# The band mask of a windowed attention: laid into the score banks by ScalarE, in place of a matmul

## The reference, cut to what matters

```
q, k = l2norm(q) * qs, l2norm(k) * ksc            # 16 heads of 64
q, k = rotary(q), rotary(k)
mask = (it < jb) | (it > jb + w) | (jb == -1)     # window w = 32
sim  = where(mask, -max, (q @ k^T) * 8)
out  = softmax(sim) @ v
x    = out @ Wo + x
x    = ffn(shift_tokens(x)) + x
```

## Time and profile before

| | |
|---|---|
| median of 3 runs | 2150.25 us (2150.19 to 2153.46) |
| span of the profiled execution | 2147.6 us |
| PE busy | 2027.4 us (94%) |
| DVE busy | 1735.7 us (81%) |
| ACT busy | 1552.4 us (72%) |
| POOL busy | 1353.9 us (63%) |
| L367, the band matmul | 384 times, 149.7 us busy, 390 ns each |
| L633, the exponentials | 1536 times, 682.4 us busy, 454 ns each |

### The profile page before, as it was taken

One profiled execution on the slowest core, in us unless ns is written; L12 is line 12 of the kernel. 1 busy time (PEld: TensorE's weight loads), 2 busy tenths in 40 slices (PEclk: granted clock), 3 DMA queues, 4 the chain that ended last, 5 costly groups with the idle time before them and its releaser, 6 DMA issues.

```text
span 2147.6 us, 44268 instructions
## 1 busy us (share of the span) xinstructions
PE 2027.4 (94%) x14352; PEld 1593.7 (74%) x14352; DVE 1735.7 (81%) x3845; ACT 1552.4 (72%) x4966; POOL 1353.9 (63%) x1884
## 2 busy tenths in 40 slices
PE   7699999899999889999999999988999999999997
PEld 5477777777777767777777777776777777777776
DVE  4688887788888678888778888867888867888876
ACT  3488887378888558888738888846888864888873
POOL 2477666466766547777547666745766664766661
PEclk8799999999999999999999999999999999999999
DMA  3000000000000010000010000001000000000000
GB/s 98 30 9 0 0 0 1 17 36 1 0 0 0 11 35 9 0 0 0 1 44 9 0 0 0 0 11 35 9 0 0 0 4 11 1 0 0 0 0 20
DMA packets 11920, 21.08 MB, mean 10 GB/s; under 512 B 1659, under 2 KB 9518, under 8 KB 11054
## 3 DMA queue, kind: packets, MB, share of 16 engines
q1 hardware_dynamic: 11822, 19.77, 2.9%
HBM read 18.72 MB, written 1.05 MB: 9 GB/s over the span
## 4 chain that ended last, share of the span: by engine, by line
PE 68%; DVE 14%; ACT 7%; issue 6%; POOL 4%; DVEq 0%; DMA 0%; ACTq 0%; SPq 0%; POOLq 0%
PE ps L371 15%; PE ps L378 7%; PE ps L351 7%; PE ps L389 7%; PE ps L359 6%; ACT pr L633 6%; PE ps L397 5%; PE ps L353 5%; PE ps L352 5%; PE ps L367 3%; PE ps L520 3%; DVE nmax L966 3%; DVE xs L924 1%; PE ps L341 1%; DVE hT L1052 1%
## 5 line engine op out<-in xcount | busy, mean ns | idle before, releaser
L633 ACT ACTIVATE pr<-ps,nbias,rn 128x128 f32<-128x128 f32 x1536 | 682.4, 454 | 204.6 <-DVE nbias L970 199.4
L784 POOL TENSOR_TENSOR pr<-pr,rsum 128x512 f32<-128x512 f32 x384 | 395.4, 1039 | 304.0 <-DVE rsum L974 304.0
L759 POOL TENSOR_TENSOR t<-t 128x512 f32<-128x512 f32 x384 | 485.1, 1273 | 65.3 <-DVE t L950 59.1
L371 PE MATMUL ps<-kT,qT 64*128 64x128 f32 x3072 | 445.1, 285 | 0.0
L371 PEld LDWEIGHTS ps<-kT,qT 64*128 64x128 f32 x3072 | 371.6, 188 | 97.5 <-issue 97.5
L966 DVE TENSOR_REDUCE nmax<-ps 128x4 f32<-128x512 f32 x384 | 258.7, 674 | 67.2 <-PE ps L371 67.1
L633 ACT ACTIVATION_READ_ACCUMULATOR pr<-ps,nbias,rn 128x1 f32 x1536 | 306.3, 199 | 0.0
L351 PE MATMUL ps<-w_hi,xt_hi 128*128 128x512 f32 x576 | 280.5, 487 | 23.1 <-DVE t L950 18.1
L948 DVE TENSOR_TENSOR t<-ps,rope 128x512 f32<-128x512 f32 x384 | 261.2, 680 | 8.7 <-ACT sq L609 8.7
L950 DVE TENSOR_TENSOR t<-ps,rope 128x512 f32<-128x512 f32 x384 | 260.5, 678 | 0.0
L934 DVE TENSOR_REDUCE ss<-sq 128x8 f32<-128x512 f32 x384 | 248.8, 667 | 3.5 <-issue 2.6
(11 more groups left out here) (116 smaller groups left out, 3173.9 us busy)
## 6 DMA issues: line engine op xcount, KB each, us to landing
wqkv<-wqkv_in SPq DMA_DIRECT2D x6, 1536.0 KB, 8.4
wo<-wo_in SPq DMA_DIRECT2D x6, 512.0 KB, 3.6
w<-w_in SPq DMA_DIRECT2D x6, 342.0 KB, 3.0
w<-w_in SPq DMA_DIRECT2D x6, 172.5 KB
x<-x_in SPq DMA_DIRECT2D x4, 256.0 KB, 4.2
out<-x SPq DMA_DIRECT2D x4, 256.0 KB, 2.3
ctx<-ctx_in SPq DMA_DIRECT2D x4, 240.0 KB, 3.8
qks<-qk_scale_in SPq DMA_DIRECT2D x6, 64.0 KB, 2.8
```

The source lines that it names most:

```text
L371: i = mm(ps[:, o, k * P:(k + 1) * P], qT[r, par, h // 2, :], kT[r, par, h // 2, :], start=False, stop=k == 3, skip_group_check=True)
L633: i = A(pr[:, g, k, :], ps[:, S_BANK[g], k * P:(k + 1) * P], ACT.Exp, bias=nbias[:, g, k:k + 1], scale=rn[:, par, g // 2, 0, 2 * k + g % 2 ...
L759: G.tensor_tensor(t1[:, c, :], t1[:, c, :], t2[:, c, :], ALU.add).then_inc(qk_added[c], 1)
L784: G.tensor_tensor(w, w, rsum[:, g, :].unsqueeze(2).broadcast_to([P, 4, P]), ALU.mult).then_inc(pr_ready[g], 1)
```

## The change

The band becomes an fp32 tensor of 128 x 512, and the bf16 band and the bf16 identity go. The band matmul of each group goes. Instead ACT copies the band into the bank right behind the group's four exponentials, after waiting for their end, and signals `band_laid[g]`; the score matmuls then add to what lies in the bank. PE waits for `band_laid` where it waited for `exp_ready`. The first band of each of the two banks in a layer is laid by `lay_first_bands`: in layer 0 ahead of the first split of x, in the others between the table load and the last squares.

```
-    ident16 = sb("ident16", [P, P], BF16)
-    band16 = sb("band16", [P, 4, P], BF16)
+    band = sb("band", [P, 4, P])
...
             def scores(l, b, par, g):
                 u = g // 2
+                if first_element(b):
+                    pe.wait_ge(band_first, l * 2 + 2)
...
-                mm(ps[:, o, :], ident16[:], band16[:].rearrange("p a k -> p (a k)"), start=True, stop=False, skip_group_check=True)
...
-                    bank_free(pe, l, i, (exp_ready[0], 2))
+                    bank_free(pe, l, i, (band_laid[0], 2))
                     scores(l, i - 2, parity, 2)
...
+                if j == 0:
+                    pe.wait_ge(band_laid[2], nth(l, B - 1))
...
                 i.then_inc(exp_ready[g], 1)
+                act.wait_ge(exp_ready[g], nth(l, b))
+                lay_band(S_BANK[g]).then_inc(band_laid[g], 1)
+
+            def lay_band(bank):
+
+                return A(ps[:, bank, :], band[:].rearrange("p a k -> p (a k)"), ACT.Copy)
+
+            def lay_first_bands(l):
+
+                if not (isinstance(l, int) and l == 0):
+                    act.wait_ge(f_h, l * (NQ * FCH))
+                lay_band(S_BANK[0]).then_inc(band_first, 1)
+                lay_band(S_BANK[1]).then_inc(band_first, 1)
...
                     nc.scalar.preload_act_table_set("natural_log_exp_and_others")
+                    lay_first_bands(n)
                     square(n, 0, 0, Q1)
                     guess_norm(n, 0, 0, 0)
```

More of the change, by code:

```diff
@@ L171, in build @@
         sems(s, 4) for s in ("s_ps", "max_ready", "bias_ready", "exp_ready", "rsum_ready", "pr_ready", "pt_ps", "pt_ready"))
+    band_laid, band_first = sems("band_laid", 4), sem("band_first")
     o_ps, o_ready = sems("o_ps", 2), sems("o_ready", 2)
@@ L433, in step @@
                 if live(i, 1):
-                    bank_free(pe, l, i, (exp_ready[3], 2), (exp_ready[1], 2))
+                    bank_free(pe, l, i, (band_laid[3], 2), (band_laid[1], 2))
                     scores(l, i - 1, 1 - parity, 1)
@@ L459, in step @@
                 if live(i, 1):
-                    bank_free(pe, l, i, (exp_ready[2], 2), (exp_ready[0], 2))
+                    bank_free(pe, l, i, (band_laid[2], 2), (band_laid[0], 2))
                     scores(l, i - 1, 1 - parity, 0)
@@ L467, in step @@
                 if live(i, 1):
-                    bank_free(pe, l, i, (exp_ready[1], 1))
+                    bank_free(pe, l, i, (band_laid[1], 1))
                     scores(l, i - 1, 1 - parity, 3)
@@ L501, in ffn_up @@
                     pe.wait_ge(f_lo, l * NQ + q + 1)
+                if j == 0:
+                    pe.wait_ge(band_laid[2], nth(l, B - 1))
                 if j == 1:
                     pe.wait_ge(x_updated, nth(l, B - 1))
+                    pe.wait_ge(band_laid[3], nth(l, B - 1))
                 if j >= 2:
@@ L523, in _ @@
             pe.wait_ge(ld_const, 80)
-            pe.wait_ge(const_ready, 8)
+            pe.wait_ge(const_ready, 7)
             cross_transpose(0)
@@ L682, in _ @@
             act.wait_ge(ld_const, 80)
-            A(ident16[:], ident, ACT.Copy).then_inc(const_ready, 1)
-            act.wait_ge(const_ready, 8)
+            act.wait_ge(const_ready, 7)
             cross_copy_inputs(0)
@@ L716, in _ @@
             nc.scalar.preload_act_table_set("natural_log_exp_and_others")
+            lay_first_bands(0)
             copy_xt(0, 0, 0)
@@ L837, in _ @@
                     split_weights(0, c + 1)
-            pool.wait_ge(const_ready, 8)
+            pool.wait_ge(const_ready, 7)
             step(0, 0, 0)
@@ L1063, in _ @@
             dve.wait_ge(ld_const, 80)
-            V.tensor_copy(band16[:], consts[:, 0:P].unsqueeze(1).broadcast_to([P, 4, P])).then_inc(const_ready, 1)
-            dve.wait_ge(const_ready, 8)
+            V.tensor_copy(band[:], consts[:, 0:P].unsqueeze(1).broadcast_to([P, 4, P])).then_inc(const_ready, 1)
+            dve.wait_ge(const_ready, 7)
             cross_normalise_x(1)
```

## The result

The changed kernel takes 2188.64 us (median of 4 runs, 2186.94 to 2196.52), the kernel before 2150.7 (2150.19 to 2153.46): a ratio of 1.019, 95% interval 1.0167 to 1.0214. It is 38 us slower. The profiled spans, from the first to the last instruction, differ by 2187.4 - 2147.6 = 39.8 us.

What follows compares the result with a forecast made beforehand. A repeating chain over GpSimd and VectorE was taken as the bound: 0.62 - 0.30 = +0.32 us a step, times 84 is +26.9, with 1.5 for the seams +28.4: 2179 us, likely range 2163 to 2195, bounds 2146 to 2211.

Steps and rivals of the forecast that it cites:

- What bounds the kernel: A repeating chain through GpSimd's norm work and VectorE operations ending with it, 18.25 us a turn, rather than TensorE.
- The copy's price: On ScalarE between exps 0 and guess_norm 0, one band copy delays the guess by 0.62 us, bounds 0.33 to 0.71.
- The saving: Ahead of the scores of g 1, the removed band matmul takes 0.30 us off a step, between 0 and 0.39.
- The g 0 matmul buys nothing: Ahead of the nbias of g 0, removing that matmul gains nothing, since GpSimd's rotate Q0 holds until 625.46.
- The step: Between successive transposes of x: +0.32 us, 18.64 in place of 18.32.
- The seams: Between layers, the two first band copies delay the square of Q1: 0.29 us five times, +1.5 us.
- TensorE's new waiting: In each step, TensorE waits some 1.2 to 1.5 us more, mostly on the transpose of x and its consumers.
- TensorE alone as the pace: Across the whole step, TensorE's list sets the time, four band matmuls save 77 us: 2073 us, chance 0.09.
- no change: Between exps 0 and guess_norm 0, the copy costs only 0.33 us and cancels the saving: 2152 us, chance 0.08.
- The second copy on the turn: Behind exps 1, a copy delays pT of g 2 and costs 0.62 us more: 2230 us, chance 0.12.
- the one behind exps 3: On ScalarE, this copy pushes the split of x to 632.18, ahead of GpSimd's 632.39: a cover of 0.2 us.
- the port opens: The copy of x and clamp_norm slip in ahead of GpSimd's work; ScalarE's list sets 18.36 us: 2155 us, chance 0.09.

Runs made afterwards that it cites:

- pool_on: Kernel before plus one 128x128 GpSimd add a step, right behind refine_norm 0: 2170.84 us, step 18.59 us.
- pool_off: Kernel before plus one 128x128 GpSimd add a step, behind normalise_p 2 where GpSimd waits: 2154.07 us, step 18.34 us.
- pe_g1: Kernel before with the band matmul of group 1 issued twice: 2170.3 us, step 18.55 us.
- pe_g3: Kernel before with the band matmul of group 3 issued twice: 2154.25 us, step 18.37 us.
- norot: Kernel before with GpSimd's rotary adds for Q0 and K0 cut from 512 to 16 columns: 2131.95 us, step 18.12 us.
- lay0: Changed kernel with the band copied only behind the exponentials of g 0; the other three groups keep their matmul: 2197.83 us, step 18.99 us.
- lay3: Changed kernel with the band copied only behind the exponentials of g 3, for group 1; the other three groups keep their matmul: 2130.99 us, step 18.11 us.
- nomask: Changed kernel with the mask left out, neither band copies nor band matmuls: 2137.96 us, step 18.10 us.
- lay123: Changed kernel without the copy behind the exponentials of g 0; the scores of g 2 keep the band matmul: 2150.96 us, step 18.11 us.
- moved03: Changed kernel with the copy behind exps 0 moved behind guess_norm 0 and that behind exps 3 behind the next step's copy of v: 2145.28 us.
- moved0: Changed kernel with only the copy behind exps 0 moved, to behind guess_norm 0: 2160.79 us, step 18.21 us.

## Why the prediction was right, point by point

- **What bounds the kernel** was right: GpSimd's stretch, with the VectorE operations that end as it does, and not TensorE (pool_on against pool_off, pe_g1 against pe_g3, norot). That POOL works without a gap there holds in every other step only; the 0.17 us between them stand before and after alike and drop out of the difference.
- **The copy's price** was forecast at 0.62, the row of an ACT copy from PSUM to SBUF, and is 0.68 in the timeline, 0.65 in lay0. The term that was off is "the next one 0.48 after its start": behind the band copy it is 0.54. The destination is not shown to be the reason. The row taken reads PSUM, the band copy reads SBUF, and the trace of the kernel before has a plain ScalarE copy of this shape between SBUF tensors, which the prediction didn't use: the next operation starts 0.54 after it as well (the median of 24 such copies).
```profile
737.12 0.63 ACT L673 ACTIVATE xhT_hi<-xhT 128x512 fp32r<-128x512 f32 x1 [2.80 <-DVE xhT L1043]
737.66 0.67 ACT L680 ACTIVATE gate<-ps,vec 114x512 f32<-114x512 f32 x1
```
With it the price would have been 0.14 + 0.54 = 0.68. The estimate by the Trainium skill (ScalarE: Activation LUTs, section "What ACT_TABLE_LOAD costs") gave 0.66.
- **The saving** was forecast at 0.30 and is 0.24 in the timeline, 0.23 in lay3. It is the 0.23 that the chain gives the matmul, and not the distance of two starts, 0.32.
- **The g 0 matmul buys nothing**: right. What it brought, 0.23 beyond the g 1 saving, went into a longer nbias (0.70). Here the rule of the Trainium skill (SBUF — State Buffer, section "Who interferes with whom") that was weighed in the prediction decided the sign.
- **The step**: forecast +0.32, measured +0.42. Both terms were off by 0.06 in the same direction. The last ten steps' 0.416 times 84 is 34.9 of the 39.8 us, where the forecast had 26.9.
- **The seams**: forecast +1.5, and 4.9 is left for all that is outside the steps. 3.3 of it stands ahead of the first transpose of x (72.73 before, 76.04 now), but nomask, which has no copy, has 76.86 there, and lay0 73.91. From the last of the 14 transposes of a layer to the first of the next layer's, the five seams changed by -3.95, +2.45, -0.42, -0.57 and -1.43, so the forecast of +0.29 each can't be read from them. The term was not separated from the spread between runs and stays unshown.
- **TensorE's new waiting**: forecast 1.2 to 1.5 us a step, mostly on the transpose of x and its consumers; it is 1.3, of which 0.7 stands ahead of that transpose.
- **The rivals**: TensorE alone as the pace, 2073 us, is refuted; no change needed a price of 0.33, and it is 0.68. The second copy on the turn, the one behind exps 1, costs nothing in lay123 and moved03 (18.11); the one behind exps 3, which was to be covered by 0.2, costs the 0.10 between moved0 and moved03. The copy of x did slip in ahead of POOL's normalise_k, as "the port opens" has it, in the first two steps of a layer: it takes 0.20 there and 1.04 in the third.

VectorE in the changed kernel, copy of x and clamp_norm in the second and third step of a layer.
```profile
473.21 0.20 DVE L942 COPY xs<-xr 128x128 f32<-128x128 f32 x1
475.80 0.53 DVE L959 TENSOR_SCALAR ss<-ss 128x16 f32<-128x16 f32 x1
...
492.05 1.04 DVE L942 COPY xs<-xr 128x128 f32 x1
```
It gained nothing, for the reason given against it: clamp_norm still ends at 476.33, with POOL's normalise_p (474.27 + 2.03 = 476.30), and the copy of v waits for that.

## What to carry to other kernels

Price an operation by its place on the turn that repeats, not by the engine's idle share: the four copies of a step took 5.3 us of work in four steps from TensorE to a ScalarE that had room, and the one that stood ahead of a short operation feeding GpSimd outweighed the rest. Look for the nearest row by source as well as by destination before pricing a new operation. Where the terms can be separated, take only the piece that carries the saving (here one copy of four, lay3) and leave the others. And follow small VectorE operations whose ends coincide with GpSimd's: what arrives earlier in front of them comes out no earlier.

## What the runs showed of the hardware

- A ScalarE copy of 128x512 fp32 from SBUF into PSUM takes 0.582 to 0.603 us (396 of them), and the next operation starts 0.54 after its start. From SBUF to SBUF that is 0.54 as well (L673 before), from PSUM to SBUF 0.48: in these rows the difference goes with the source, and no cheaper destination shows.
- A VectorE product of 128x4 took 0.16 with GpSimd idle or on tiny operands, and 0.70 in the turn shown, up to 1.00 in the changed kernel as a whole, while GpSimd ran a 128x512 add; a 128x128 copy took 0.20 to 1.10.
- TensorE's mean granted clock varied from run to run of one kernel, 0.963 to 0.977 in nomask, whose times lay 20 us apart with it; in its profiled run and in the kernel before, stretches at the lower level of 1.2 GHz stand at the seam shown.
- An added POOL operation of 0.40 us cost 0.25 on average, since it covered a gap of about 0.2 that appears in every other step.
